# Gene weights split into float16 parts and turned by DMA, with every engine's order written anew

## The reference

```python
q = (x @ Wq).reshape(b, n, 32, 16); k, v = jnp.split(ctx @ Wkv, 2, axis=-1)   # x is layer-normed
q, k = apply_axial_rope(q, pos), apply_axial_rope(k, pos)
w = jax.nn.softmax(jnp.einsum('bqhd,bkhd->bhqk', q, k) * scale, axis=-1)
x = x + jnp.einsum('bhqk,bkhd->bqhd', w, v).reshape(...) @ Wout + bout
# feed-forward, xn = rms-norm of the layer-normed x
logits = jnp.einsum('btd,gd->btg', xn, Wc) / jnp.clip(temperature, 0.1)       # 1024 genes
top_vals, top_idx = jax.lax.top_k(logits, 32)
expr_w = jax.nn.softmax(top_vals, axis=-1)
expressed = jnp.einsum('btk,btkc->btc', expr_w, genes[top_idx])               # genes: 1024 x 64
down = jnp.tanh(expressed @ Wd.T); up = expressed @ Wu.T
x = x + down * xn * up * 0.1
```

## Time and profile before

| | |
|---|---|
| median of three executions | 516.35 us |
| the profiled execution | 516.95 us |
| its span, first to last instruction | 515.0 us |
| matmuls on PE | 441.8 us busy (86%) |
| DVE | 410.0 us busy (80%) |
| ACT | 279.4 us busy (54%) |
| POOL | 261.1 us busy (51%) |
| mean granted TensorE clock | 0.963 of 2.4 GHz |
| first and last `normalise` (L977) | 60.4 and 462.7 us |

### The profile page before, as it was taken

One profiled execution on the slowest core, in us unless ns is written; L12 is line 12 of the kernel. 1 busy time (PEld: TensorE's weight loads), 2 busy tenths in 40 slices (PEclk: granted clock), 3 DMA queues, 4 the chain that ended last, 5 costly groups with the idle time before them and its releaser, 6 DMA issues. The chain is left out here.

```text
span 515.0 us, 11003 instructions
## 1 busy us (share of the span) xinstructions
PE 441.8 (86%) x3829; PEld 280.2 (54%) x3829; DVE 410.0 (80%) x661; ACT 279.4 (54%) x424; POOL 261.1 (51%) x262
## 2 busy tenths in 40 slices
PE   3546776978999899899999999999989899888795
PEld 3232554545556566465656565656556565565353
DVE  5781874497989898798888888888898988875993
ACT  3431838264655656465656565657475757354122
POOL 4423718173556556484838393939392929111110
PEclk9956889989999999999999999999999999989999
DMA  5893231725172626244343434343434342310101
GB/s 195 264 198 91 50 74 39 118 23 114 33 124 53 123 55 106 71 76 98 71 102 68 101 69 102 71 103 71 102 74 83 71 86 44 83 23 20 41 1 43
DMA packets 115665, 42.93 MB, mean 83 GB/s; under 512 B 107040, under 2 KB 109104, under 8 KB 115632
## 3 DMA queue, kind: packets, MB, share of 16 engines
q1 hardware_dynamic: 114624, 41.45, 37.8%
q10 hardware_dynamic: 1008, 1.05, 0.6%
HBM read 12.86 MB, written 4.19 MB: 33 GB/s over the span
## 5 line engine op out<-in xcount | busy, mean ns | idle before, releaser
L1229 PE MATMUL gene<-wcT_h,yT 128*128 128x512 f16 x256 | 81.9, 382 | 1.4 <-DMA yT<-y_hl 1.4
L1031 DVE MAX8 top<-stage_b 128x8 f32<-128x1024 f32 x64 | 78.4, 1225 | 3.6
L1039 DVE MATCH_REPLACE8 stage_b<-top,stage_b 128x1024 f32<-128x1024 f32 x64 | 77.5, 1211 | 0.2
L432 POOL TENSOR_TENSOR x_hl<-xn,x_hl 128x512 f16<-128x512 f32 x16 | 18.8, 1175 | 80.3 <-issue 40.7
L472 POOL TENSOR_TENSOR rstd<-var,minus_half 128x1 f32<-128x1 f32 x16 | 8.8, 548 | 93.1 <-DVE var L1003 86.6
L1229 PE MATMUL dense<-wq_h,xT 128*128 128x512 f16 x128 | 43.1, 397 | 7.0 <-DMA xT<-x_hl 4.9
L1229 PE MATMUL gene<-wcT_l,yT 128*128 128x512 f16 x128 | 48.8, 381 | 0.0
L443 POOL TENSOR_TENSOR stage_b<-stage_b,cos_t 128x512 f32<-128x512 f32 x31 | 39.5, 1275 | 15.4 <-issue 11.0
L669 ACT ACTIVATE stage_b<-gene 128x512 f32<-128x512 f32 x32 | 18.8, 590 | 47.8 <-PE gene L1229 47.6
L964 DVE TENSOR_REDUCE row_max<-score_a 128x8 f32<-128x1024 f32 x32 | 39.0, 1219 | 6.5 <-PE score_a L1296 6.2
L444 POOL TENSOR_TENSOR stage_b<-stage_b,sin_t 128x512 f32<-128x512 f32 x31 | 43.6, 1406 | 0.0
(11 more groups left out here) (163 smaller groups left out, 1065.1 us busy)
## 6 DMA issues: line engine op xcount, KB each, us to landing
x_ring<-x_dram SPq DMA_DIRECT2D x16, 256.0 KB, 3.0
out_dram<-x_ring SPq DMA_DIRECT2D x16, 256.0 KB, 2.1
ctx_sb<-ctx_dram SPq DMA_DIRECT2D x16, 128.0 KB, 2.1
wc_raw<-L_ffn_Wc_dram SPq DMA_DIRECT2D x4, 512.0 KB, 6.8
stage_b<-L_xattn_Wq_dram ACTq DMA_DIRECT2D x4, 256.0 KB, 5.2
stage_a<-L_xattn_Wkv_dram SPq DMA_DIRECT2D x2, 512.0 KB, 8.0
stage_a<-L_xattn_Wout_dram SPq DMA_DIRECT2D x1, 1024.0 KB, 9.5
genes_sb<-L_ffn_genes_dram SPq DMA_DIRECT2D x2, 256.0 KB, 4.6
```

Source lines behind the costliest of these rows:

```text
L1031: nc.vector.max(top[:, 8 * n:8 * n + 8], logit if n == 0 else rest).then_inc(s_top[n], 1)
L1039: nc.vector.match_replace(rest, top[:, 8 * n:8 * n + 8], logit if n == 0 else rest, REMOVED).then_inc(s_rem[n], 1)
L1229: last = nc.tensor.matmul(out, lhs(k), rhs(k), start=(n == 0), stop=(n == steps - 1))
```

## The change

1. **Gene weights.** The PE transposes and the two ACT reads of them go. ACT writes a float16 high part (`w_hi`), POOL the low part (`w_lo`, 128 x 1024), into `w_hl`, and SP turns both with one DMA transpose of 2048 columns (`turn_w`). The exp is scaled up by 2^15 by way of its bias.
2. **Expression.** The genes are scaled by a power of two and split into float16 parts once; `express` is 16 float16 matmuls (8 blocks, high and low of the weights). Both parts of `expressed` are made for all 128 rows (`eT_h`, `eT_l`), and `down_up` has three matmuls for each half.
3. **First logits half in two pieces.** `logits0(t, 0)` stands between `transpose_o` and `transpose_attn`, `logits0(t, 1)` a round later before `project_k`.
4. **Orders.** All five programs are ordered anew. The last rounds get 20 and 50 `keep_busy` where there were 7 and 5 ahead of `express`, and the 33 of another place go.
5. **Opening.** x of tile 0 is loaded in two halves by two queues, the k rotation and the split of Wk move from POOL to DVE, the turn of x of tile 1 comes ahead of the late loads, and there are more `keep_warm`.

The core of the diff:

```diff
+            def turn_w(t):
+                ready = t + 1
+                hold(sp)
+                sp.wait_ge(s_w_h, ready)
+                sp.wait_ge(s_w_l, ready)
+                if not first(t):
+                    sp.wait_ge(s_eT, t)
+                sp.dma_start_transpose(wT.rearrange("p (m t) -> p m t", t=P),
+                                       w_hl[:].rearrange("p l d -> p (l d)")).then_inc(s_wT, 16)
...
+            def w_lo(t):
+                pool.wait_ge(s_gw, t + 1)
+                pool.wait_ge(s_w_h, t + 1)
+                if not first(t):
+                    pool.wait_ge(s_wT, 16 * t)
+                pool.tensor_tensor(w_hl[:, 1], gene_w, w_hl[:, 0], ALU.subtract).then_inc(s_w_l, 1)
...
-            def read_wT(t, n):
-                act.wait_ge(s_wT[n], t + 1)
-                nc.scalar.activation(gene_wT[:, n * 512:(n + 1) * 512], gene[:, n * 512:(n + 1) * 512],
-                                     ACT.Copy).then_inc(s_wTr[n], 1)
+            def w_hi(t):
+                act.wait_ge(s_gw, t + 1)
+                if not first(t):
+                    act.wait_ge(s_wT, 16 * t)
+                nc.scalar.activation(w_hl[:, 0], gene_w, ACT.Copy).then_inc(s_w_h, 1)
...
-            def transpose_w(t, n):
-                pe.wait_ge(s_gw, t + 1)
-                    last = nc.tensor.transpose(gene[:, g * P:(g + 1) * P], gene_w[:, g * P:(g + 1) * P], ident[:])
...
+            def express(t):
+                pe.wait_ge(s_wT, 16 * (t + 1))
...
-                for g in range(GK):
-                    last = nc.tensor.matmul(gene[:, 0:P], genes_sb[:, g], gene_wT[:, g * P:(g + 1) * P],
-                                            start=(g == 0), stop=(g == GK - 1))
+                for g in range(2 * GK):
+                    last = nc.tensor.matmul(gene[:, 0:P], genes_hl[:, g % GK], wT[:, g * P:(g + 1) * P],
+                                            start=(g == 0), stop=(g == 2 * GK - 1))
...
-                nc.tensor.matmul(gene[:, cols], eT_hl[:], wduT_h[:, cols], start=True, stop=False)
-                nc.tensor.matmul(gene[:, cols], eT_hl[:], wduT_l[:, cols], start=False,
+                nc.tensor.matmul(gene[:, cols], eT_h[:], wduT_h[:, cols], start=True, stop=False)
+                nc.tensor.matmul(gene[:, cols], eT_h[:], wduT_l[:, cols], start=False, stop=False)
+                nc.tensor.matmul(gene[:, cols], eT_l[:], wduT_h[:, cols], start=False,
                                  stop=True).then_inc((s_dn, s_upp)[n], 1)
```

More of the change, by code:

```diff
@@ L360, in iteration @@
             def iteration(t0, t1, t2, t3, t4, t5, t6, t7):
+                if t7 is not None:
+                    turn_w(t7)
+                if t4 is not None:
+                    shift(t4, 0)
+                    shift(t4, 1)
+                if t5 is not None:
+                    turn_y(t5)
+                if later(t3):
+                    turn(t3, 1)
                 if t3 is not None:
@@ L363, in iteration @@
                 if first(t3):
+                    load_bout()
+                    next_x(2)
+                    turn_x(1)
                     load_late()
-                    next_x(2)
+                if later(t2) and not (isinstance(t2, int) and t2 == 1):
+                    turn_x(t2)
+                if later(t1, 1):
+                    next_ctx(t1)
+                if t7 is not None:
+                    store(t7)
                 if later(t0, 2):
                     next_x(t0)
[L368 to L380, removed]
             turn_x(0)
@@ L506, in iteration @@
                     add_bout(0)
-                if t7 is not None and not last_tile(t7):
-                    finish(t7)
+                if later(t1, 1):
+                    ln1(t1)
+                if t6 is not None:
+                    w_lo(t6)
+                if t4 is not None:
+                    ln2(t4)
+                if later(t2):
+                    rope(t2, 1)
+                    rope_sum(t2, 1)
+                    rope(t2, 0)
+                    rope_sum(t2, 0)
+                    split_lo(t2, 1)
+                    split_lo(t2, 0)
+                    add_bout(t2)
+                if t6 is not None and not last_tile(t6):
+                    gate(t6)
             ln1(0)
             x_lo(0)
-            wk_lo(0)
-            rope(0, 1)
-            rope_sum(0, 1)
-            split_lo(0, 1)
             ln1(1)
@@ L750, in iteration @@
[L750 to L761 removed]
+                if first(t2):
+                    wout_hi()
+                if t2 is not None:
+                    neg_max_hi(t2)
@@ new lines, in iteration @@
+                if later(t2) and not (isinstance(t2, int) and t2 == 1):
+                    project_q(t2)
+                if t3 is not None:
+                    scoresT(t3, 0)
+                    scoresT(t3, 1)
+                if isinstance(t3, int) and t3 == 1:
+                    transpose_job(8)
+                    transpose_job(9)
+                if isinstance(t6, int) and t6 == TILES - 3:
+                    keep_busy(7)
+                if isinstance(t6, int) and t6 == TILES - 2:
+                    keep_busy(20)
@@ new lines, in iteration @@
+                if last_tile(t6):
+                    keep_busy(50)
+                if t6 is not None:
+                    express(t6)
+                if t3 is not None:
+                    values(t3, 0)
+                    scoresT(t3, 2)
+                    scoresT(t3, 3)
+                    values(t3, 1)
+                if isinstance(t3, int) and t3 == 1:
+                    spread(GENE)
+                if t3 is not None:
+                    values(t3, 2)
+                if isinstance(t6, int) and t6 == TILES - 3:
+                    keep_busy(6)
@@ new lines, in iteration @@
+                if isinstance(t6, int) and t6 == TILES - 2:
+                    keep_busy(4)
+                if last_tile(t6):
+                    keep_busy(3)
+                if t6 is not None:
+                    down_up(t6, 0)
+                if t3 is not None:
+                    values(t3, 3)
+                if first(t3):
+                    transpose_job(0)
+                    transpose_job(1)
+                if t6 is not None:
+                    down_up(t6, 1)
+                if t3 is not None:
+                    transpose_o(t3)
```

503 lines of the change are left out of this document (249 added, 254 removed).

## The result

The changed kernel took 501.5 us (median of 4 runs, 500.1 to 503.4), the kernel before 517.4 beside it: a ratio of 0.971 with a 95% interval of 0.966 to 0.975. The forecast was 504.6 with a range of 494 to 516. Its sum came out nearly right because two of its terms missed in opposite directions: the opening by +6.1 us, the distances by -7.8. The profiled execution has a span of 501.4 us, against 515.0 before.

The account below looks back on a forecast made before the run. PE and DVE, both nearly full, wait for each other once a tile. 515.0 - 4.6 - 11.9 + 4.8 = 503.3 us span, 505.2 with 1.95 around it; less the profiled run's 0.6, 504.6; range 494 to 516.

Parts of the forecast that it names:

- the opening: Start to first `normalise`, 60.4 us before: PE's 4.93 us wait for `xT` of tile 1 goes, -4.6 us.
- the distances: The 15 intervals between successive `normalise` operations, 402.3 us before: sum 390.4, -11.9 us.
- PE's term: PE's work per tile: transposes -1.09, `express` -0.95, `down_up` +0.5, together -1.5 us.
- A: DVE's stretch from `normalise` to the residual: 6.3 us, 8.2 before.
- B: DVE's stretch from the residual to the end of the fourth group maximum: 6.8 us, 5.6 before.
- C: DVE's stretch from the fourth group maximum to the next `normalise`: 11.7 us, 12.2 before.
- The lock: In the loop, DVE's negated top and `norm1_shift` are held by a POOL operation: 0.7 us a period, up to 1.1.
- the second rival: DVE's mask and `y_lo` wait for POOL as well, 0.6 us a tile: 512 us in total; chance 0.14.
- Ending: After the last `normalise`, 52.3 us before: mask to `express` 9.3 instead of 3.3, in all +4.8 us.
- the third (slower): SP's `turn_w` holds up the writes of the maxima, PE bounds at 26.6: 15 us more, 520; chance 0.11.
- The first: Rival: DVE's small operations fall between POOL's and are not held; period 24.8, total about 495 us; chance 0.18.
- The fourth: Rival: the opening gives nothing, another wait holds the first `scoresT` until 50; total 509 us; chance 0.07.

Follow-up runs that it names:

- Experiments 2 and 3: 2: changed kernel with seven idle products ahead of each k projection from tile 2, 514.6 us; 3: gene part in the orders of the kernel before, 527.1 us.
- experiment 1: The changed kernel with three one-column DVE operations (two shifts, negated top) written as tensor_scalar: 494.2 us, ratio to before 0.955.
- experiment 8: The changed kernel with the edits of experiment 1, Experiment 4 and experiment 6, plus POOL's gate moved ahead of its addition of bout: 487.5 us.
- Experiment 4: The changed kernel with the load of x of tile 2 moved ahead of the turn of k of tile 0 on SP: 498.5 us.
- experiment 6: The kernel of Experiment 4 with PE's projection of q of tile 1 moved behind the transposed maximum of tile 0: 491.7 us.

## Why the prediction was right, and where not

- **What bounds** was right: two nearly full engines that wait for each other. Experiments 2 and 3 show it from both sides. The gene part with its 1.6 us less of PE is worth 0.05 us in the old orders, and 1.5 us of PE cost 1.19 when given back in the new ones, 0.76 of it in a wait behind PE and 0.23 by the mask that is then held.
- **PE's term**: -1.5 forecast, 24.97 to 23.61 us busy, so -1.4. `express` 1.07 against 1.1.
- **DVE's chain** A + B + C was put at 24.8 without the lock; experiment 1 runs at 24.73, with A 6.5 (6.3 forecast), B 6.6 (6.8) and C 11.6 (11.7). In two of those five periods C ends with a wait for PE.
- **The lock**: 0.7 taken with up to 1.1 allowed; removing it gave 0.67. Of the two operations named only `norm1_shift` was held (1.13 to 1.16 us in 11 of 16 tiles); the negated top was held in the last two tiles alone. The period forecast at 25.5 came out at 25.3 to 25.6. The rule of the Trainium skill (GPSIMD Engine Reference, Specifications) on instructions "with two SBUF inputs" was doubted for the mask, as no row showed it held. By that rule the mask had to be exposed, and it is: 2.1 to 2.4 us in 4 of 16 tiles after the change, in 11 of 16 in experiment 8. Experiment 1 agrees with it too. What decides is which operation begins first, by tenths of a microsecond, so the second rival's case did occur, in four tiles. Its price of 0.6 a tile was too high for the mask: two of the four lie in periods of 25.60 and 25.40 among neighbours of 25.35. `y_lo`, the other operation it names, took 0.80 to 1.01 us in seven tiles and 0.67 to 0.70 in the others.
- **The step that failed: the opening**, -4.6 forecast, +1.5 measured. The working followed PE's queue and priced a wait that did go. Its own lower bound spoke of another wait in its place, and that came on DVE: the statistics of tile 2 ahead of the first maximum, with their load now behind the turn. I had counted that statistic as a filler of stretch A in the loop, and didn't ask whether its input is there in the first round. Experiment 4 brings back 2.2 to 4.5 us of it, experiment 6 another 4.0.
- **A term mis-sized: the distances**, -11.9 forecast, -19.7 measured. Not the loop: the last nine were given 25.4 each, and seven of them took 25.39 on average; the two last came at 24.2 and 24.5. The four rounds ahead of the loop took 101.8 instead of 105.2: their 26.3 was the time before less the old hold of `norm2_shift`, which is indeed gone (0.14 in all 16 tiles), but without the 0.6 that a loop period gains. I put 4 x 0.6 = 2.4 of the 3.4 down to that; no run tests it. The entry of the loop was 1.7 us over a period before, with this wait of PE for the turn of q in it, which I took to stay:

```profile
207.93 0.40 PE L1296 MATMUL score_a<-kT,qT 64*128 64x128 f16 x8 [1.62 <-DMA qT<-parts]
```

With the new order of SP there is no such wait, and the entry is 25.6.
- **Ending**: 57.1 forecast, 56.9 measured, and part of that is luck. The terms that the working names add up to +6.0 (mask to `express` +6.0, from there on -0.65, the combine +0.7); "with the rest +4.8" takes off 1.2 more without a row for it. Measured, the last `normalise` to the last mask takes 40.2 as before, so the +0.7 did not come; mask to `express` takes 8.4 instead of 9.3, the turn having landed 3.7 after its issue at 489.38, which is +5.1; and what follows is 0.5 shorter.
- **Rivals**: the third (slower) did not occur, but SP came free for the writes of the maxima just as these were ready (283.40 and 283.06), without the 1 to 2 us of slack. The first needs the locks to miss, which was not the case. Its period of 24.8 is what experiment 1 measured (24.7). That its total of 495 came out too (494) is partly luck: it carries the opposite misses of opening and distances, and the 9 us between it and the forecast were 7.4. The fourth did occur in the opening (first `scoresT` at 52.64, later than its 50), with distances shorter than forecast.

## What to carry to other kernels

When an order is rewritten, walk every moved instruction through the first round too: an operation whose input is old news in the loop can be the first to want a load in the opening. When two engines share the path, count what one edit gives only together with the order it needs; alone the gene part gave 0.05 us of 26. Before removing a wait, look what the next operation waits for: DVE's 1.00 for the gate was followed by a wait for PE, and taking it away gave nothing. And write a small vector operation so that it reads one tensor and scalars where the form allows it: here it cost 0.06 us and took a hold of 1 us away.

## What the runs showed of the hardware that was not expected

- The hold of the earlier trace rows was met by a DVE operation of 1024 columns as well: with two tensors in SBUF and begun 0.05 to 0.1 us after one of POOL, it took 2.28 in place of 1.23 us, and one of one column 1.14 in place of 0.15. Both are held until about 0.1 us before the end of POOL's operation. POOL is held in the other case: 2.14 in place of 1.29. The same arithmetic as `tensor_scalar`, its second operand a scalar pointer, was never held in 16 tiles, 13 of which began inside an operation of POOL.
- Removing a wait can lead into a hold: moving the gate took away a wait of 1.00 us and put a hold of 1.05 in its place.
- Issuing one transposing DMA took SP 1.6 us in some executions of the opening and 3.78 or 5.36 in others, and whatever SP has behind it waits as well. The opening varies for other reasons too: the first `normalise` of one and the same kernel came at 53.00 and 55.24, with that issue at 1.65 and 1.64 but begun at 25.24 and 27.34.
